# Local attention: one exponential more ahead of the copy of an older chunk's outputs on ScalarE

## The chip, the cores and the metric

The kernel runs on one core of a Trainium2 chip. The metric is device time in microseconds. The engines are called PE (TensorE, matmuls; its weight loads are listed as PEld), DVE (VectorE), ACT (ScalarE), POOL (GpSimd) and SP (SyncE).

## The reference

A small two-layer network on 4 images. The first stage (`tok`) makes 1024 tokens of 64 features per image by a short Fourier transform of patches. Then come local attention, a mixture of experts, full attention over each image, and a second mixture with a capacity, each after a layernorm and added to the stream. Only local attention matters here, per image:

```python
q = x @ wq.T                      # 16 heads of 64
kv = x @ wkv.T                    # one head of keys and values
k, v = (kv[..., :64], kv[..., 64:])
q = _rmsnorm(_rope(q), q_norm_w)
k = _rmsnorm(_rope(k), k_norm_w)
mask = (cols <= rows) & (rows - cols <= 128)
scores = jnp.einsum('bqgtd,bqgsd->bqgts', q, k) / sqrt(64)
scores = jnp.where(mask[None, None, None], scores, NEG)
attn = jax.nn.softmax(scores, axis=-1)
out = jnp.einsum('bqgts,bqgsd->bqgtd', attn, v)
return out.transpose(0, 3, 1, 2, 4).reshape(Bx, Tx, 1024) @ wo.T
```

## The kernel before

Each engine has its own written-out program, and engines wait for each other through counting semaphores; nothing is planned by a scheduler. The stages are setup, then for each of the 4 images `project` and `windowed` as one stage, then `experts`, `full` and `finish`. A barrier of all engines stands between stages.

`windowed` does local attention. The 1024 tokens of an image are cut into 32 chunks of 32 query rows. A chunk sees 160 keys (its own 32 and the 128 before). The 16 heads are handled as 4 groups q = 0 to 3 of 4 heads, so that a chunk's scores are 4 tiles of 128 x 160 in two PSUM banks, banks 0 and 1 for even chunks and 2 and 3 for odd ones. What the engines do in a chunk:

- PE, `scores` (L645 the mask, L649 the products): writes the chunk's scores. It waits until all four exponentials of the chunk two before are done, since they read the same banks (L634).
- DVE, L739 and L742: the maximum of each row, then the bias of the exponential from it (`bias_ready`). ACT waits for the bias at L789.
- ACT, L796: four ACTIVATEs with Exp, one per q, from PSUM to `probs`. Each also sums its row, and each is followed in the trace by an ACTIVATION_READ_ACCUMULATOR that stores the sum and counts up `exp_done`.
- DVE, L759: the reciprocal of the four sums, when all four exponentials are done. POOL, L775 and L777: the probabilities multiplied by it (`scaled`).
- PE, `turn` (L667): transposes the probabilities, of the 128 older keys and of the 32 own ones. It works on the chunk three before the one whose scores were just made. DVE, L751, copies them out of PSUM (`pT_ready`); the last three chunks are shared by DVE (L755) and ACT (L804).
- PE, `values` (L684 for the older keys, L681 for the own ones): the products with the values, in banks 6 and 7, four chunks behind the scores. It counts up `pv_done`. Before it writes the two banks for chunk c, it waits for `oT_ready` to reach c (L673), i.e. for the copy of chunk c - 1's outputs.
- ACT, `outputs` (L784): the copy of a chunk's outputs from banks 6 and 7 to `oT` in SBUF. It waits for `pv_done` (L783) and counts up `oT_ready`. Within ACT's slot for chunk c it copies chunk c - 4.

The order of the work is that of the programs. PE goes over n = 0 to 35 with scores(n), turn(n - 3), values(n - 4), in this order. DVE goes over n with maximum and bias of chunk n, the copy of the transposed chunk n - 3, the reciprocal of chunk n - 1. ACT goes over the chunks with its four exponentials, and from chunk 4 on with one copy between two of them. After ACT's loop, the outputs of the last four chunks are copied one by one (L800 to L805). Then PE multiplies all outputs by `wo` (L715), and the stage ends with transposes and additions. The loads of local attention's data are done by then, and the loop issues no DMA.

ACT's loop, with the placement of the copy at L793 and L794:

```python
for c in range(CHUNKS):
    a.wait_ge(S["bias_ready"], c + 1)
    if c >= 3:
        a.wait_ge(S["transposed"], c - 2)
    for q in range(NQ):
        if q == 2 and c >= 4:
            outputs(c - 4)
        e, hh = divmod(q, 2)
        nc.scalar.activation(probs[:, c % 3, q, :], ...
```

Of the kernel before, what the change touches and what calls it, by code (L numbers as in the profile page):

```python
# [80 lines left out]
def program(nc, inp, out_rows, sent_rows):  # L81
    with ExitStack() as ctx:
# [205 lines left out]
        def turned_scalar(a, at):  # L288

            a.wait_ge(S["xT_psum"], 1)  # L290
            nc.scalar.activation(xT[:, 0:HALF // 2], bank[at][:, 0:HALF // 2], ACT.Copy)
# [322 lines left out]
        def turned_half(c, r):  # L614

            return pT[:, c % 2, :].rearrange("p (q r t) -> p r q t", r=2, t=D)[:, r]

        def bank_of_half(r):

            return bank[4 + r][:, 0:(NQ + 1) * D].rearrange("p (q t) -> p q t", t=D)  # L620

        def windowed(block, b):
# [157 lines left out]
            @block.scalar  # L780
            def _(a):
                def outputs(c):
                    a.wait_ge(S["pv_done"], c + 1)  # L783
                    nc.scalar.activation(oT[:, :, CHUNK * c:CHUNK * (c + 1)].rearrange("p (h a) t -> p h a t", h=2),  # L784
                                         ps[:, 6:8, 0:P].rearrange("p h (a t) -> p h a t", t=CHUNK),
                                         ACT.Copy).then_inc(S["oT_ready"], 1)

                for c in range(CHUNKS):
                    a.wait_ge(S["bias_ready"], c + 1)  # L789
                    if c >= 3:  # L790
                        a.wait_ge(S["transposed"], c - 2)
                    for q in range(NQ):
                        if q == 2 and c >= 4:  # L793
                            outputs(c - 4)  # L794
                        e, hh = divmod(q, 2)
                        nc.scalar.activation(probs[:, c % 3, q, :],  # L796
                                             bank[2 * (c % 2) + e][:, SPAN * hh:SPAN * hh + SPAN], ACT.Exp,
                                             bias=small[:, c % 4, 1, q:q + 1], scale=rq[:, c, e, hh:hh + 1],
                                             accum_out=small[:, c % 4, 2, q:q + 1]).then_inc(S["exp_done"], 1)
                for c in range(CHUNKS - 4, CHUNKS):  # L800
                    if c + 1 < CHUNKS:
                        a.wait_ge(S["transposed"], c + 2)
                        a.wait_ge(S["pv_done"], c)
                        nc.scalar.activation(turned_half(c + 1, 1), bank_of_half(1), ACT.Copy).then_inc(S["pTr_ready"], 1)  # L804
                    outputs(c)  # L805
                a.wait_ge(S["out_done"], 1)
                nc.scalar.activation(outT, bank[0][:], ACT.Copy).then_inc(S["out_kept"], 1)
                if b + 1 < IMAGES:
                    turned_scalar(a, 1)
# [866 lines left out]
```

## Time and profile before

| | us |
|---|---|
| median of 3 runs | 902.27 (901.76 to 904.99) |
| the profiled execution | 902.57 |
| its span | 900.6 |
| PE busy | 728.4 (81%) |
| DVE busy | 606.4 (67%) |
| ACT busy | 449.2 (50%) |
| POOL busy | 429.0 (48%) |
| loop of local attention, image 0, first to last exponential | 84.1 to 153.4 |
| last exponential of image 3 | 519.4 |

The loop of local attention stands four times in the span, once per image. Busy times are sums of an engine's records, and records can overlap. Busy PE time is modelled and says little of how near PE is to its peak. Times in a timeline are from the start of the span.

### The profile page before, as it was taken

The page shows a single profiled execution, that of the slowest core. Times are in us where ns is not written, and L with a number is a line of the kernel's source. Part 1 is how long each engine was busy: PE and PEld are TensorE (multiplying, and loading weights), DVE is VectorE, ACT ScalarE, POOL GpSimd, SP SyncE. Part 2 cuts the span into 40 slices and gives each one's busy share as a digit, 9 for nine tenths or more (in the row PEclk, how much of TensorE's full clock was granted, in tenths as well). Part 3 has the DMA queues.
Part 4 walks back from the last instruction along what each step waited for, and adds up shares of the span by engine and source line. Part 5 has one row for each costly group of instructions (what it writes and reads, how often), then busy time and mean ns, then how long its engine had stood idle before and what let it go on. Part 6 is the DMA issues. An engine that isn't in the chain of part 4 may idle for free. (4 is left out here: it accounts for less than half of the span.)

```text
span 900.6 us, 21152 instructions
## 1 busy us (share of the span) xinstructions
PE 728.4 (81%) x8196; PEld 474.9 (53%) x8196; DVE 606.4 (67%) x1209; ACT 449.2 (50%) x1405; POOL 429.0 (48%) x556
## 2 busy tenths in 40 slices
PE   6699999899998989988689979987899986405850
PEld 6243776436774447764267734773577763403630
DVE  0378887598884988876878836676577759421980
ACT  0024999228993359972299925311666650201100
POOL 0655665275662656643656612662033230472675
PEclk9989999999999999999999998997999997556975
DMA  6453000170000810001200000008000004017000
GB/s 234 137 201 77 3 3 3 69 209 2 3 3 1 239 38 3 2 3 31 60 2 3 3 1 1 2 2 112 7 3 2 2 2 130 25 47 129 9 20 14
DMA packets 60009, 41.31 MB, mean 46 GB/s; under 512 B 51760, under 2 KB 57389, under 8 KB 59124
## 3 DMA queue, kind: packets, MB, share of 16 engines
q1 hardware_dynamic: 57462, 33.03, 14.6%
q10 hardware_dynamic: 144, 4.19, 1.2%
q0 software_dynamic: 2304, 2.74, 0.9%
q8 instruction: 66, 1.08, 0.5%
q14 instruction: 33, 0.27, 0.1%
HBM read 25.44 MB, written 7.15 MB: 36 GB/s over the span
## 5 line engine op out<-in xcount | busy, mean ns | idle before, releaser
L796 ACT ACTIVATE work<-ps,small,rq 128x160 f32<-128x160 f32 x512 | 243.3, 487 | 32.3 <-DVE small L742 31.8
L775 POOL TENSOR_TENSOR work<-work,small 128x512 f32<-128x512 f32 x128 | 133.3, 1041 | 123.6 <-DVE small L759 123.6
L739 DVE TENSOR_REDUCE ps<-ps 128x4 f32<-128x640 f32 x128 | 106.5, 832 | 40.6 <-PE ps L649 39.0
L796 ACT ACTIVATION_READ_ACCUMULATOR work<-ps,small,rq 128x1 f32 x512 | 105.2, 205 | 0.0
L649 PE MATMUL ps<-kT,big 64*128 64x160 f32 x1024 | 97.9, 311 | 0.0
L751 DVE COPY pT<-ps 128x640 f32<-128x640 f32 x116 | 95.5, 824 | 0.5 <-issue 0.5
L684 PE MATMUL ps<-pT,vwin 128*64 128x128 f32 x1024 | 84.2, 282 | 10.1 <-ACT big L784 2.4
L273 PE MATMUL ps<-xT,s_proj_w 64*128 64x512 f32 x288 | 76.9, 650 | 13.3 <-PEq L213 7.5
L609 POOL TENSOR_TENSOR big<-prod 128x1024 f32<-128x1024 f32 x28 | 65.8, 2362 | 26.2 <-DVE prod L576 26.0
L649 PEld LDWEIGHTS ps<-kT,big 64*128 64x128 f32 x1024 | 76.1, 191 | 0.1
L684 PEld LDWEIGHTS ps<-pT,vwin 128*64 128x64 f32 x1024 | 56.7, 136 | 24.0 <-issue 20.0
L526 ACT ACTIVATE big<-ps 128x1024 f32<-128x1024 f32 x32 | 32.8, 1024 | 62.5 <-DVE prod L576 57.5
L1561 POOL DMA_INDIRECT out<-big x40 | 44.0, 1100 | 32.4 <-DVE big L1531 20.5
L667 PE MATMUL ps<-s_ident,work 64*128 64x64 f32 x1024 | 55.3, 226 | 3.2 <-DVE pT L751 2.5
L681 PE MATMUL ps<-pT,vrem 32*64 32x128 f32 x1024 | 57.3, 293 | 0.0
L273 PEld LDWEIGHTS ps<-xT,s_proj_w 64*128 64x128 f32 x288 | 28.0, 197 | 53.4 <-issue 28.9
L1175 DVE TENSOR_REDUCE h<-ps 128x1 f32<-128x1024 f32 x32 | 39.1, 1225 | 23.1 <-PE ps L1082 23.1
L784 ACT ACTIVATE big<-ps 128x256 f32<-128x256 f32 x128 | 48.7, 380 | 10.6 <-PE ps L681 10.6
L1554 POOL DMA_INDIRECT sent_rows<-big,xb x32 | 31.5, 986 | 43.7 <-DVEq L1505 34.3
L667 PEld LDWEIGHTS ps<-s_ident,work 64*128 64x128 f32 x1024 | 47.8, 139 | 8.1 <-POOL pTr_own L777 4.2
L777 POOL TENSOR_TENSOR pTr_own<-work,small 128x128 f32<-128x128 f32 x128 | 51.3, 401 | 0.0
L1207 POOL TENSOR_TENSOR sum_off<-sum_off,hl 128x64 f32<-128x64 f32 x32 | 10.3, 321 | 79.9 <-DVE hl L1195 79.8
(284 smaller groups left out, 1407.0 us busy)
## 6 DMA issues: line engine op xcount, KB each, us to landing
xb<-in_x SPq DMA_DIRECT2D x3, 4096.0 KB, 13.2
xb<-in_x ACTq DMA_DIRECT2D x1, 4096.0 KB, 17.7
vrem<-hl SPq DMA_DIRECT2D x64, 64.0 KB, 2.1
sent_rows<-empty_row SPq DMA_DIRECT2D x8, 325.0 KB
s_proj_w<-in_proj_w SPq DMA_DIRECT2D x1, 1536.0 KB, 6.3
big<-sent_rows SPq DMA_DIRECT2D x5, 264.0 KB, 5.2
big<-sent_rows SPq DMA_DIRECT2D x5, 256.0 KB, 4.5
xb<-in_ffn_w SPq DMA_DIRECT2D x1, 1028.0 KB, 4.7
```

Source lines behind the costliest of these rows:

```text
L273: ins = nc.tensor.matmul(bank[banks + w][:], proj_w[half_rows(w), cols], xT[half_rows(w), :], start=True, stop=True)
L609: g.tensor_tensor(dst, first, second, ALU.add).then_inc(S["rot_done"], 1)
L649: ins = nc.tensor.matmul(tiles[e][:, hh, :], qT[half_rows(e), c, 4 * hh:4 * hh + 4, :].rearrange("p a t -> p (a t)"), kT[half_rows(e), CHU ...
L667: ins = nc.tensor.transpose(bank[4 + r][:, D * q:D * q + D], src, ident[half_rows(r), half_rows(r)])
L681: ins = nc.tensor.matmul(o, vrem[r, c, :], pT[r, c % 2, NQ * P:], start=False, stop=True, tile_position=(CHUNK * q, D * e), skip_group_che ...
L684: nc.tensor.matmul(o, vwin[:, c, :], pT[:, c % 2, P * q:P * q + P], start=True, stop=True, skip_group_check=True)
L739: ch.step(v.tensor_reduce(row_max(c), ps[:, s_banks(c), 0:2 * SPAN].rearrange("p e (h k) -> p e h k", h=2), X, ALU.max))
L751: v.tensor_copy(pT[:, c % 2, :].rearrange("p (q r t) -> p r q t", r=2, t=D), ps[:, 4:6, 0:(NQ + 1) * D].rearrange("p r (q t) -> p r q t", ...
L775: g.tensor_tensor(probs[:, c % 3, :, 0:P], probs[:, c % 3, :, 0:P], bc(small[:, c % 4, 3, :], P), ALU.mult)
L777: g.tensor_tensor(own[:, c % 2, :].rearrange("p (q k) -> p q k", q=NQ), probs[:, c % 3, :, P:SPAN], bc(small[:, c % 4, 3, :], CHUNK), ALU. ...
L784: nc.scalar.activation(oT[:, :, CHUNK * c:CHUNK * (c + 1)].rearrange("p (h a) t -> p h a t", h=2), ps[:, 6:8, 0:P].rearrange("p h (a t) -> ...
L796: nc.scalar.activation(probs[:, c % 3, q, :], bank[2 * (c % 2) + e][:, SPAN * hh:SPAN * hh + SPAN], ACT.Exp, bias=small[:, c % 4, 1, q:q + ...
```

## The change

The copy of chunk c - 4's outputs moves within ACT's slot for chunk c: it stood between the second and the third exponential and now stands between the third and the fourth.

```diff
                     for q in range(NQ):
-                        if q == 2 and c >= 4:
+                        if q == 3 and c >= 4:
                             outputs(c - 4)
                         e, hh = divmod(q, 2)
```

`outputs`, its wait and its count are unchanged, and so are all other engines' programs.

## Rows read from the trace of the kernel before

**Rows 1.** The page: PE's granted clock in 40 slices, tenths.

```profile
PEclk9989999999999999999999998997999997556975
```

**Rows 2.** Busy time by stretch; PE, PEld, DVE, ACT, POOL (instructions), PEclk, DMA share, GB/s.

```profile
96.00:149.00 53.00, 51.52 (x876) 40.09 (x876) 44.17 (x99) 53.00 (x219) 33.98 (x50) 1.00 0.01 2
```

**Rows 3.** Who waited for whom, 96 to 149 us: total, times, longest.

```profile
DVE ps L739 <- PE ps L649: 8.4, 25, 0.5
...
PEld ps L645 <- ACT work L796: 4.1, 24, 0.2
```

**Rows 4.** Timeline of image 0's loop: start, us, engine and line; [idle before, releaser].

```profile
116.46 0.10 PEld L645 LDWEIGHTS ps<-window_mask,row_of_t 64*128 64x128 bf16 x2 [0.17 <-ACT work L796]
...
117.12 0.38 ACT L784 ACTIVATE big<-ps 128x256 f32<-128x256 f32 x1
...
117.32 0.14 PEld L667 LDWEIGHTS ps<-s_ident,pTr_own 64*128 64x128 f32 x2
...
117.38 0.49 ACT L796 ACTIVATE work<-ps,small,rq 128x160 f32<-128x160 f32 x1
...
117.61 0.45 PEld L684 LDWEIGHTS ps<-pT,vwin 128*64 128x64 f32 x8
...
117.84 0.49 ACT L796 ACTIVATE work<-ps,small,rq 128x160 f32<-128x160 f32 x1
...
118.21 0.22 ACT L796 ACTIVATION_READ_ACCUMULATOR work<-ps,small,rq 128x1 f32 x1
118.22 0.21 PEld L681 LDWEIGHTS ps<-pT,vrem 32*64 32x64 f32 x8 [0.17 <-issue]
...
118.60 0.10 PEld L645 LDWEIGHTS ps<-window_mask,row_of_t 64*128 64x128 bf16 x2 [0.17 <-ACT work L796]
...
119.35 0.38 ACT L784 ACTIVATE big<-ps 128x256 f32<-128x256 f32 x1
...
120.35 0.16 DVE L742 SCALAR_TENSOR_TENSOR small<-ps,rq 128x4 f32<-128x4 f32 x1
...
120.55 0.49 ACT L796 ACTIVATE work<-ps,small,rq 128x160 f32<-128x160 f32 x1
...
121.49 0.38 ACT L784 ACTIVATE big<-ps 128x256 f32<-128x256 f32 x1
```

**Rows 5.** Timeline of the first chunks of image 0's loop, in the same columns.

```profile
89.96 0.21 ACT L796 ACTIVATION_READ_ACCUMULATOR work<-ps,small,rq 128x1 f32 x1
...
90.21 0.10 PEld L645 LDWEIGHTS ps<-window_mask,row_of_t 64*128 64x128 bf16 x2 [1.18 <-ACT work L796]
...
91.07 0.14 PEld L667 LDWEIGHTS ps<-s_ident,pTr_own 64*128 64x128 f32 x2
...
91.28 0.42 PEld L684 LDWEIGHTS ps<-pT,vwin 128*64 128x64 f32 x8
...
91.81 0.22 ACT L796 ACTIVATION_READ_ACCUMULATOR work<-ps,small,rq 128x1 f32 x1
...
91.86 0.21 PEld L681 LDWEIGHTS ps<-pT,vrem 32*64 32x64 f32 x8 [0.17 <-issue]
...
92.24 0.10 PEld L645 LDWEIGHTS ps<-window_mask,row_of_t 64*128 64x128 bf16 x2 [0.17 <-ACT work L796]
```

**Rows 6.** Timeline of the last chunks of image 0, in the same columns.

```profile
152.11 0.38 ACT L784 ACTIVATE big<-ps 128x256 f32<-128x256 f32 x1
...
152.60 0.45 PEld L684 LDWEIGHTS ps<-pT,vwin 128*64 128x64 f32 x8 [0.20 <-issue]
...
153.74 0.39 ACT L784 ACTIVATE big<-ps 128x256 f32<-128x256 f32 x1
153.86 0.36 PEld L667 LDWEIGHTS ps<-s_ident,work 64*128 64x128 f32 x8 [0.44 <-POOL pTr_own L777]
...
154.35 0.42 PEld L684 LDWEIGHTS ps<-pT,vwin 128*64 128x64 f32 x8
```

**Rows 7.** The line L784 over the whole trace: idle time before it (us, times).

```profile
  PE ps L681: 10.6, 13
```

## The prediction

> **What bounds the kernel now.** I went from the page to one stretch of local attention, and there from one handoff to the next.
>
> The page's clock line says that TensorE's clock was granted in full, but for a few dips, until the last third [rows 1]. The chain that ended last covers the final stage, so the question is what sets the pace of a chunk here. The stretch 96 to 149 us lies inside the chunk loop of image 0: ScalarE is busy 53.00 of 53.00 us, TensorE 51.52, VectorE 44.17 [rows 2]. ScalarE looks like the bound. But its records overlap (an accumulator read runs under the next ACTIVATE), so "full" can hide a wait of some hundredths. The chain of waits says so: 24 times the load for the next scores waited 0.17 us, and 25 times VectorE's maximum waited for the scores, 8.4 us in all [rows 3]. Something comes round in a ring.
>
> The timeline shows the ring [rows 4]. ScalarE's copy in chunk 15 (outputs of chunk 11) starts at 117.12 and takes 0.38, to 117.50. TensorE's values product starts at 117.61, 0.11 later; its loads end with L681's at 118.22 + 0.21 = 118.43. The scores of chunk 17 start at 118.60, 0.17 later; then come maximum and bias (120.35), chunk 17's first exponential at 120.55, 1.95 after the scores' start, and its copy at 121.49. From copy to copy over two chunks: 121.49 - 117.12 = **4.37 us** = 0.38 + 0.11 + 0.82 + 0.17 + 1.95 + 0.94. Each handoff begins when the one before ends.
>
> Two links could be chance, so I looked for each where it stands apart.
> - Copy to values. `values` waits for oT_ready of the chunk before, i.e. for the copy. The first one of an image has no copy before it, and its load follows the last transposing load by 0.07 (91.07 + 0.14 to 91.28) [rows 5]. In the loop that gap is 0.15 (117.32 + 0.14 to 117.61) and ends 0.11 after the copy [rows 4]; so it does at the image's end (152.11 + 0.38 to 152.60) [rows 6]. The copy ends this wait, by some 0.08 us.
> - Values to scores. At 118.60 both possible releasers ended together: L681's loads at 118.43, and the fourth exponential's accumulator read at 118.21 + 0.22 = 118.43 [rows 4]. The profile names the exponential. The loop's head parts them: where only the exponential is awaited, the scores' load starts about 0.05 after it (89.96 + 0.21 to 90.21); at 92.24 it starts 0.21 after the exponential (92.03) and again 0.17 after L681's loads (92.07) [rows 5]. So the 0.17 belongs to the products before, the ring goes through the copy, and the ring of the exponentials alone has 0.12 us to spare.
>
> **The change part by part.** It removes and adds no instruction. 28 copies per image (chunks 4 to 31), 112 in all, go behind the third exponential; the last four of each image, after the loop, stay. The moved step issues no DMA and passes no queue; only ScalarE's order changes.
>
> 1. The third exponential starts where the copy did, and the copy one exponential later. That step is 117.84 - 117.38 = 0.46 us [rows 4]. The fourth exponential starts and ends as before, since the same work stands before it. Worth 0: nothing waits for the third alone, the scores and the reciprocal wait for all four.
> 2. The copy's own wait for its product. The product whose loads end at 118.43 is copied at 119.35 [rows 4]; before this line ScalarE sat idle only 13 times of 128, 10.6 us in all [rows 7], nearly all of it behind the loop. No wait comes and none goes: 0.
> 3. The copy ends 0.46 later after its chunk's first exponential, so the next values product starts 0.46 later. Queued behind it on TensorE are the scores of the chunk after, with no slack at the 0.17 link. VectorE's maximum, the bias and the first exponential follow at the same 1.95, each waiting for the one before; VectorE idles before its maximum already [rows 3]. A round of the ring grows from 4.37 to **4.83 us**, a chunk from 2.19 to 2.42.
> 4. What is late next: the transposing products stand before the values in TensorE's order. They end 1.00 after the scores' start (116.46 to 117.46) [rows 4] and could let the values go 0.07 later, at 1.07; the values now start at 1.15 and will at 1.43. That leaves 0.36 us, so they don't matter; the gap is new idle time of TensorE.
> 5. How many rounds: chunk 4's copy delays chunk 6's scores, 6's delays 8's, up to 28's and 30's; the odd chunks likewise from 5 to 31. That is **13 rounds on each side**, interleaved and not added. 13 x 0.464 (the 0.46 with a little for the steps of 0.48 among them) = 6.03 us per image.
> 6. The end of the image. The last copy in the loop (152.11) also moves by 0.46, so the values at 152.60 go to 153.07, their copy from 153.74 to 154.20, and the transposes at 153.86 wait for the values' loads (153.07 + 0.82 + 0.17 = 154.06). The next values start 0.11 after the copy's end at 154.59, so at 154.70 instead of 154.35 [rows 6]. What follows is serial: 0.35 per image.
>
> Sum: 4 x (6.03 + 0.35) = **25.5 us**. The term that could be off is a round's growth. At the top 0.48, the longest step between exponentials: 4 x (6.24 + 0.35) = 26.4. At the bottom, if the 0.17 were the exponential's release and the scores could follow the values' loads with no gap, 0.46 - 0.17 = 0.29: 4 x (3.77 + 0.2) = 15.9.
>
> The profiled execution took 902.57 us with a span of 900.6, 2.0 around it, and stands 0.3 above the median of 902.27. By its own time the sum is 928.1; by the median **927.8**. I take 0.464 and not the bottom, because its row at 92.24 is a direct reading.
>
> Between two groups of loads on different rows of the array the timeline shows 0.17, from L684 to L681 and from L681 to the scores. The Trainium skill (TensorE: Matmul & The Clock Gate, "The mechanism" in Part 3) says that weight loads are pulled ahead of matmuls in flight when row groups don't conflict. By that rule the scores' loads would slip in under the values' matmuls and the sum would lie near the bottom, 15.9; the gap of 0.17 at the one place where it can be told speaks for 25.5.
>
> **The rivals.**
> - *The link to the scores gives way*: the exponential, not the products, released them. For: both end at 118.43, and the profile names it. Against: the 0.21 at 92.24 [rows 5]. Time 902.3 + 15.9 = 918.2.
> - *ScalarE is the bound, and its order doesn't matter.* For: 53.00 of 53.00 us [rows 2]. As a mechanism: four exponentials and a copy cost the same in any order, so the chunk stays 2.19, time 902.3. Against: they need only 0.48 + 3 x 0.46 + 0.26 = 2.12 us, and each first exponential starts within 0.05 of the bias's end. The Trainium skill (Perfetto Trace Analysis, "Identifying the Most-Contended Engine") takes the engine of highest occupancy for the one to optimize, and for ScalarE calls occupancy a fair measure; that is this rival's reading.
> - *Faster: in the loop the copy stalls the third exponential*, hidden under the overlapping records. Moved back, it would find its product finished and the chunk shrink toward 2.13: 112 x 0.06 = 6.7 us less, 895.6. It decides from the point where the product ends less than 0.05 us before the copy. Against: its loads end 0.9 us before, and rows 7.
> - *The clock.* TensorE idles 0.23 us more per chunk. Its full clock held through the loop [rows 2]; the dips stand at image borders and at the end [rows 1]. Borders move by 6 us, so dips may come or go, a few us either way. If the lower level (1.2 GHz) took hold of a loop, the 0.82 and a part of the 1.95 would lengthen and the time pass 935. Nothing at these idle shares suggests it.
>
> **How the numbers follow.** Ring through the copy, at full growth: 86%. Link gives way: 6%. No change: 4%. Faster: 1%. Clock falls: 3%, with the forecast's sign. The range takes in the first two: 917 at the bottom (918.2 less 1 for dips), 931.5 at the top (902.3 + 26.4, and 3 for dips and the spread of the runs, whose highest is 904.99). A measurement tells about 0.5%, 4.5 us, from no change: faster 1%, same 4%, slower 95%.
>
> **What would show it.** In the loop: copy to copy 4.83 us over two chunks; values still 0.11 after the copy; scores still 0.17 after L681's loads, but 0.6 after the accumulator read; ScalarE waiting for the bias (L742) some 100 times at 0.15 to 0.2 us and busy below 95% of the stretch; L684 waiting for ACT L784 by some 0.4 us each; VectorE's wait before L739 up by 0.23 each. It is wrong if copy to copy stays 4.37 or is near 4.66, or if the time appears outside the loop.

## The result and the profile after

| | before | after |
|---|---|---|
| median, us (4 runs each) | 902.01 (901.44 to 904.99) | 927.81 (926.29 to 929.47) |
| profiled execution, us | 902.57 | 926.86 |
| its span, us | 900.6 | 924.0 |

The ratio is 1.028, with a 95% interval of 1.026 to 1.030: slower, by 25.8 us. The forecast was 927.8 us.

The same view as [rows 4], a stretch of image 0's loop after the change; the columns are start and duration in us, engine and line, and in brackets the idle time before and its releaser:

```profile
118.88 0.47 ACT L796 ACTIVATE work<-ps,small,rq 128x160 f32<-128x160 f32 x1
...
119.14 0.10 PEld L645 LDWEIGHTS ps<-window_mask,row_of_t 64*128 64x128 bf16 x2 [0.17 <-ACT work L796]
...
119.80 0.38 ACT L784 ACTIVATE big<-ps 128x256 f32<-128x256 f32 x1
...
120.29 0.45 PEld L684 LDWEIGHTS ps<-pT,vwin 128*64 128x64 f32 x8
...
120.43 0.22 ACT L796 ACTIVATION_READ_ACCUMULATOR work<-ps,small,rq 128x1 f32 x1
...
120.91 0.21 PEld L681 LDWEIGHTS ps<-pT,vrem 32*64 32x64 f32 x8 [0.17 <-issue]
...
121.09 0.48 ACT L796 ACTIVATE work<-ps,small,rq 128x160 f32<-128x160 f32 x1 [0.45 <-DVE small L742]
...
121.29 0.10 PEld L645 LDWEIGHTS ps<-window_mask,row_of_t 64*128 64x128 bf16 x2 [0.17 <-issue]
...
122.49 0.38 ACT L784 ACTIVATE big<-ps 128x256 f32<-128x256 f32 x1
...
122.99 0.45 PEld L684 LDWEIGHTS ps<-pT,vwin 128*64 128x64 f32 x8 [0.66 <-issue]
...
123.12 0.22 ACT L796 ACTIVATION_READ_ACCUMULATOR work<-ps,small,rq 128x1 f32 x1
...
123.23 0.48 ACT L796 ACTIVATE work<-ps,small,rq 128x160 f32<-128x160 f32 x1
...
123.98 0.10 PEld L645 LDWEIGHTS ps<-window_mask,row_of_t 64*128 64x128 bf16 x2 [0.17 <-ACT work L796]
...
124.64 0.38 ACT L784 ACTIVATE big<-ps 128x256 f32<-128x256 f32 x1
```

Read it as a ring. The copy at 119.80 ends at 120.18; the values start 0.11 later at 120.29; their loads end at 120.91 + 0.21 = 121.12; the scores start 0.17 later at 121.29. By then the fourth exponential's accumulator read had been over since 120.65, for 0.64 us. The chunk's first exponential starts at 123.23, 1.94 after the scores, and its copy at 124.64, another 1.41 later. Copy to copy over two chunks is 124.64 - 119.80 = 4.84 us = 0.38 + 0.11 + 0.83 + 0.17 + 1.94 + 1.41, where it was 4.37 [rows 4]. Every link has its old length to within 0.01 us but the last one, from first exponential to copy, which was 0.94. The profile still names the exponential as releaser of the scores at 123.98, although its accumulator read was over at 123.12 + 0.22 = 123.34, 0.64 us before: with several waits, the releaser that is named need not be the one that counts.

The next rows cover the same stretch of 53 us as [rows 2] and [rows 3]: busy us of PE, PEld, DVE, ACT and POOL, then clock and DMA; below it who waited for whom (total, times, longest). The third block is for the copy's line over the whole trace, as in [rows 7]: ScalarE's idle time before it, and who waited for it (us, times). The last line is the same wait in the kernel before.

```profile
96.00:149.00 53.00, 46.55 (x792) 36.26 (x790) 39.89 (x88) 48.08 (x198) 30.40 (x45) 1.00 0.01 2
```

```profile
DVE ps L739 <- PE ps L649: 12.5, 22, 1.0
...
PE ps L684 <- ACT big L784: 6.0, 11, 0.6
ACT work L796 <- DVE small L742: 4.9, 11, 0.5
```

```profile
  PE ps L681: 12.9, 16
who waited for it (us, times):
  PE ps L684: 32.3, 60
```

```profile
  PE ps L684: 2.4, 4
```

ScalarE is busy 48.08 of 53 us and no longer looks full. It waits for the bias 11 times at 0.45 us, and TensorE waits for the copy (L684 <- L784) 60 times in the whole trace, 32.3 us in all, where it was 4 times and 2.4 us before, once at the end of each image.

From the start of image 0's first exponential to the start of its last the loop took 68.73 us before (84.11 to 152.84) and takes 74.77 now:

```profile
84.00 0.48 ACT L796 ACTIVATE work<-ps,small,rq 128x160 f32<-128x160 f32 x1 [7.24 <-DVE small L742]
...
158.77 0.49 ACT L796 ACTIVATE work<-ps,small,rq 128x160 f32<-128x160 f32 x1
```

That is 6.04 us more. (The 153.4 and the 519.4 of the table before the change belong to the accumulator reads of those last exponentials; by starts they are 152.84 and 519.0.) The four images' loops in the two traces, counted in this way, and the last copy of an image behind its last exponential:

| | before, us | after, us | more |
|---|---|---|---|
| loop of image 0 | 68.73 | 74.77 | 6.04 |
| loop of image 1 | 68.89 | 74.73 | 5.84 |
| loop of image 2 | 68.70 | 74.72 | 6.02 |
| loop of image 3 | 69.25 | 77.27 | 8.02 |
| last exponential to last copy, images 0 to 2 | 5.87 or 5.88 | 6.25 or 6.26 | 0.38 |
| the same, image 3 | 5.99 | 6.25 | 0.26 |

### The profile page after: what moved, and what is told of

Its sections match the earlier page's. It is cut to its first block and busy times, and to the rows that moved or that the text cites. A ratio compares the mean times of both kernels' runs of the same rounds, so it can differ in the third digit from the quotient of the medians.

```text
span 924.0 us, 21152 instructions
## 1 busy us (share of the span) xinstructions
PE 732.5 (79%) x8196; PEld 480.4 (52%) x8196; DVE 606.1 (66%) x1209; ACT 449.9 (49%) x1405; POOL 427.6 (46%) x556
## 5 line engine op out<-in xcount | busy, mean ns | idle before, releaser
L796 ACT ACTIVATE work<-ps,small,rq 128x160 f32<-128x160 f32 x512 | 243.5, 484 | 55.9 <-DVE small L742 55.5
L684 PE MATMUL ps<-pT,vwin 128*64 128x128 f32 x1024 | 84.7, 283 | 37.1 <-ACT big L784 32.3
L273 PE MATMUL ps<-xT,s_proj_w 64*128 64x512 f32 x288 | 76.9, 650 | 13.3 <-PEq L213 7.5
L684 PEld LDWEIGHTS ps<-pT,vwin 128*64 128x64 f32 x1024 | 57.2, 137 | 51.3 <-issue 46.2
L681 PE MATMUL ps<-pT,vrem 32*64 32x128 f32 x1024 | 57.6, 294 | 0.0
L784 ACT ACTIVATE big<-ps 128x256 f32<-128x256 f32 x128 | 49.1, 384 | 12.9 <-PE ps L681 12.9
L576 DVE TENSOR_TENSOR prod<-ps,s_rope_cos 128x1024 f32<-128x1024 f32 x32 | 39.0, 1219 | 13.4 <-PE ps L273 11.7
```

The lines of the kernel that those rows point to most:

```text
L273: ins = nc.tensor.matmul(bank[banks + w][:], proj_w[half_rows(w), cols], xT[half_rows(w), :], start=True, stop=True)
L681: ins = nc.tensor.matmul(o, vrem[r, c, :], pT[r, c % 2, NQ * P:], start=False, stop=True, tile_position=(CHUNK * q, D * e), skip_group_che ...
L684: nc.tensor.matmul(o, vwin[:, c, :], pT[:, c % 2, P * q:P * q + P], start=True, stop=True, skip_group_check=True)
L796: nc.scalar.activation(probs[:, c % 3, q, :], bank[2 * (c % 2) + e][:, SPAN * hh:SPAN * hh + SPAN], ACT.Exp, bias=small[:, c % 4, 1, q:q + ...
```

## The experiments

The theory: the pace is set by a ring from ScalarE's copy over the values and the scores, behind them in TensorE's order, back to ScalarE. Its rivals: the exponentials' own release of the scores; ScalarE's amount of work; a fixed price per moved copy; the amount of TensorE's work. Periods below are copy to copy over two chunks, read off the timeline of image 0's loop.

### One place earlier

```diff
-                        if q == 2 and c >= 4:
+                        if q == 1 and c >= 4:
```

> The copy stands between the first and the second exponential, one place earlier than in the kernel before. Ring through the copy: that ring would shrink by 0.46 to 3.91 us per two chunks, so the next ring binds. It is the one of the exponentials: 1.95 from the scores' start to the first exponential, 1.67 to the fourth, 0.59 to the end of its accumulator read, 0.05 to the next scores: 4.25 us. 13 x 0.12 x 4 = 6 us less: about 896 us. The scores then start 0.05 after the accumulator read. If the exponential is what released the scores with 0.17 in the kernel before: the ring stays 4.37 and the time 902. If only ScalarE's work counts: 902 too.

Measured: ratio 0.995 (0.992 to 0.998); median 905.7 beside 909.3 for the kernel before on that chip. The timeline of this kernel's loop:

```profile
116.21 0.40 ACT L784 ACTIVATE big<-ps 128x256 f32<-128x256 f32 x1
...
116.80 0.17 PEld L667 LDWEIGHTS ps<-s_ident,pTr_own 64*128 64x128 f32 x2
...
117.05 0.42 PEld L684 LDWEIGHTS ps<-pT,vwin 128*64 128x64 f32 x8
...
117.40 0.53 ACT L796 ACTIVATE work<-ps,small,rq 128x160 f32<-128x160 f32 x1
...
117.63 0.21 PEld L681 LDWEIGHTS ps<-pT,vrem 32*64 32x64 f32 x8 [0.17 <-issue]
...
117.77 0.25 ACT L796 ACTIVATION_READ_ACCUMULATOR work<-ps,small,rq 128x1 f32 x1
...
118.07 0.10 PEld L645 LDWEIGHTS ps<-window_mask,row_of_t 64*128 64x128 bf16 x2 [0.23 <-ACT work L796]
...
120.49 0.40 ACT L784 ACTIVATE big<-ps 128x256 f32<-128x256 f32 x1
```

The scores start 0.05 after the accumulator read (118.02 to 118.07) and 0.23 after L681's loads (117.84). So the exponential now releases them, and it takes 0.05 to do so, not 0.17. The values follow the last transposing load by 0.08 (116.97 to 117.05) and wait for no copy. The period is 120.49 - 116.21 = 4.28 us against 4.25 expected: the first rival, which had the ring stay at 4.37, falls. The 0.03 lies in the fourth exponential and its read, 0.62 us here (117.40 to 118.02) and 0.59 in [rows 4]. A chunk now takes 2.14 us, 0.02 more than the 2.12 of ScalarE's own work, so this run parts the exponentials' ring from ScalarE's work by no more than that.

The gain, 3.7 us by the medians and 0.5% by the ratio, is smaller than the 6 us expected. The loops of images 0 to 2 are 1.28, 1.20 and 1.33 us shorter than in the kernel before, but that of image 3 is 0.92 longer (70.17 against 69.25). The last section shows why.

On another chip, beside two of the others:

> The kernel of e1_second once more, beside the changed kernel and e3's on one chip. By its loops (67.98 us against 69.22 in image 0) it should be 4 x 1.2 = 5 us shorter than the kernel before, 0.5%, and 30 us shorter than the changed kernel.

Measured: 0.9957 (0.994 to 0.9975), 899.5 us beside 902.3, some 3 to 4 us where 5 were expected. The expectation multiplied image 0's gain by four, and image 3's loop again did not share in it (70.12 us). The gain is small but clear of the noise, so this placement beats both kernels.

### Ahead of the first exponential

```diff
-                        if q == 2 and c >= 4:
+                        if q == 0 and c >= 4:
```

> The copy stands ahead of the first exponential. Ring through the copy: now the copy comes before its values product is done. The product of the same round ends 2.14 us after the scores' start and is seen 0.06 later, so the copy starts at 2.20 instead of being free at 1.95, and the first exponential at 2.46; from there 1.40 to the fourth, 0.59 and 0.05: 4.50 us per two chunks, 0.13 more than before: 13 x 0.13 x 4 = 7 us more, about 909. A plain rule that earlier is better would give 896 or less; a rule that ScalarE's order doesn't matter gives 902.

Measured: 1.015 (1.010 to 1.019), 923.9 us beside 909.3: longer, as expected, but by twice the size. The timeline:

```profile
118.04 0.38 ACT L784 ACTIVATE big<-ps 128x256 f32<-128x256 f32 x1
...
119.78 0.45 PE L681 MATMUL ps<-pT,vrem 32*64 32x128 f32 x8
119.88 0.16 DVE L742 SCALAR_TENSOR_TENSOR small<-ps,rq 128x4 f32<-128x4 f32 x1
...
120.37 0.38 ACT L784 ACTIVATE big<-ps 128x256 f32<-128x256 f32 x1
120.65 0.48 ACT L796 ACTIVATE work<-ps,small,rq 128x160 f32<-128x160 f32 x1
```

The bias is ready at 120.04, but the copy now stands in front of the exponential and waits for its product, whose modelled end is 120.23; it starts 0.14 after that, not the 0.06 that the expectation took from the end of an image; why is not shown. The period is 4.55 us (from 115.82 to 120.37; the chunk between starts its copy at 118.04), 0.18 over the kernel before. That gives 4 x 13 x 0.18 = 9.4 us of the 13.6 measured. The rest lies in the loops too: those of images 0 to 2 are 2.7 to 2.9 us longer than before (71.45 us in image 0), of which 13 rounds of 0.18 explain 2.3, and that of image 3 is 4.9 longer (74.16 against 69.25), 13.3 in all. "Earlier is better" holds only up to the point where the copied product is late.

### Behind the fourth exponential

```diff
-                        if q == 2 and c >= 4:
-                            outputs(c - 4)
...
+                    if c >= 4:
+                        outputs(c - 4)
```

> The copy stands behind the fourth exponential, one place later than in the changed kernel. Ring through the copy: 0.46 more again, 5.30 us per two chunks, so 4 x (13 x 0.93 + 0.7) = 51 us over the kernel before: 953. If the exponentials' ring were what grew, it would be shorter here, since the copy no longer stands ahead of the fourth: about 896 to 902. If it is ScalarE's work alone: 902, as in any order.

Measured: 967.0 us beside 909.3, 1.067 (1.061 to 1.073). The single runs spread from 958.7 to 973.3. The timeline:

```profile
114.72 0.39 ACT L784 ACTIVATE big<-ps 128x256 f32<-128x256 f32 x1
...
115.22 0.45 PEld L684 LDWEIGHTS ps<-pT,vwin 128*64 128x64 f32 x8 [1.12 <-issue]
...
116.22 0.10 PEld L645 LDWEIGHTS ps<-window_mask,row_of_t 64*128 64x128 bf16 x2 [0.17 <-ACT work L794]
...
120.03 0.39 ACT L784 ACTIVATE big<-ps 128x256 f32<-128x256 f32 x1
```

In this kernel the exponentials are L794. The next copy of the same ring starts at 120.03: 5.31 us, where 5.30 was expected. No copy stands between the first and the fourth exponential any more, so by the links of [rows 4] the ring of the exponentials is down to 1.95 + 1.40 + 0.59 + 0.05 = 3.99 us, and yet the time is the longest of all placements. So that ring and ScalarE's amount of work are both out. The total was higher than the loops explain, hence:

> The kernel of e3_behind once more. Its loops were 11.8 us longer per image, 47 us in all, and with the image's end about 50 (5.5%), but the time was 6.7% longer. If the rest was that chip's, the ratio is now near 1.055; if it belongs to the kernel (a clock lowered outside the loops, for one), it is again near 1.067 and the profile shows where.

Measured: 953.7 us beside 902.3, 1.056 (1.053 to 1.060), near the 1.055 that the loops and the images' ends give. The surplus of the first measurement is in part explained and in part open. Its profiled execution (958.7 us, 1.054 times the 909.3) has the same loops as this one (80.54 us in image 0), and behind image 3's last exponential it took 387.1 us against 381.0. The other kernels traced on that chip took 386.6 to 389.0 there as well, so those 6 us are the chip's, which fits the kernel before at 909.3 there and 902.3 here. They don't raise the ratio. What does are two executions of 972.65 and 973.32 us with a mean granted clock of 0.892, where the two shorter ones had 0.917 and 0.910. On the second chip one of four was of that kind (968.95 us at 0.893). None of them was traced, so whether this placement makes them more likely is not shown.

### The changed kernel on that chip

> The changed kernel itself, so that the placements are compared on one chip: loops 6.04 us longer per image than in the kernel before, 25 us in all, 1.028. Against e4_even_only's 1.024 it tells whether moving half of the copies costs all but the whole.

Measured: 928.25 us, 1.028 (1.026 to 1.031). The placements on one scale; the first row's ratio is from another chip:

| the copy stands | period, us | ratio to before |
|---|---|---|
| before the 1st | 4.55 | 1.015 |
| before the 2nd exponential | 4.28 | 0.996 |
| before the 3rd (the kernel before) | 4.37 | 1 |
| before the 4th (the change) | 4.84 | 1.028 |
| behind the 4th | 5.31 | 1.056 |

### Half of the move

```diff
-                        if q == 2 and c >= 4:
+                        if q == 3 - c % 2 and c >= 4:
```

> Only the copies in even chunks stand between the third and the fourth exponential, those in odd chunks stay between the second and the third: half of the move. Two rings run interleaved, one through the even and one through the odd chunks, and ScalarE takes the chunks in order, so the faster waits for the slower. Ring through the copy: the even ring grows to 4.84 and drags the odd one, so nearly the whole price is paid: 4 x 13 x 0.464 = 24 us, about 926. If each moved copy costs 0.23 us by itself, half of them cost half: 915.

Measured: 1.024 (1.020 to 1.028), 932.1 us beside 909.3. Rows of the timeline:

```profile
114.03 0.10 PEld L645 LDWEIGHTS ps<-window_mask,row_of_t 64*128 64x128 bf16 x2 [0.17 <-ACT work L796]
...
114.18 0.41 ACT L784 ACTIVATE big<-ps 128x256 f32<-128x256 f32 x1
...
114.88 0.15 PEld L667 LDWEIGHTS ps<-s_ident,pTr_own 64*128 64x128 f32 x2
...
115.10 0.42 PEld L684 LDWEIGHTS ps<-pT,vwin 128*64 128x64 f32 x8
...
115.97 0.48 ACT L796 ACTIVATE work<-ps,small,rq 128x160 f32<-128x160 f32 x1 [0.45 <-DVE small L742]
...
117.38 0.39 ACT L784 ACTIVATE big<-ps 128x256 f32<-128x256 f32 x1
...
119.03 0.41 ACT L784 ACTIVATE big<-ps 128x256 f32<-128x256 f32 x1
...
122.22 0.38 ACT L784 ACTIVATE big<-ps 128x256 f32<-128x256 f32 x1
```

Both parities run at the long period: the moved ones 122.22 - 117.38 = 4.84, the unmoved 119.03 - 114.18 = 4.85. A price per moved copy would have given 1.014. Image 0's loop takes 74.75 us, as with all copies moved (74.77). What stays away is the price at the image's end: chunk 31 is odd, its copy is not moved, and the last copy follows the last exponential by 5.91 us, near the 5.87 of the kernel before.

The expectation laid the dragging on ScalarE, which takes the chunks in order. The rows put most of it on TensorE. The unmoved copy of chunk 13 ends at 114.59, but the values start at 115.10, not 0.11 but 0.51 later, and 0.07 after the last transposing load (114.88 + 0.15 = 115.03). Those transposes stand behind the scores of 114.03 in TensorE's order, and the scores belong to the slower ring. That is 0.40 of the 0.47 us that the slower ring is longer. ScalarE's own order adds less than 0.1: the unmoved chunk 15 has its bias at 117.97 and starts its first exponential at 118.10, behind the fourth of chunk 14, where 0.04 behind the bias is the rule.

### Fewer products in the ring

In the changed kernel and in the kernel before, the same edit; the count `pv_done` moves to the last product that is left:

```diff
-                    for own_keys in range(2):
+                    for own_keys in range(1):
```

> The changed kernel, with the values products of the own keys (L681) left out, so the outputs lack the part of a chunk's own 32 keys. Ring through the copy: the products in the ring shrink from 0.82 to 0.45 us of loads, the ring from 4.84 to 4.46 us per two chunks (the 0.17 behind them taken as before): 13 x 0.38 x 4 = 20 us less than the changed kernel, about 908. If the products aren't in what binds, 928 stays; if the clock had fallen for idleness it would be worse still.

> The kernel before, with the same products (L681) left out, so the outputs lack the same part. Ring through the copy: here the ring through the copy falls to 3.99, but the exponentials' ring of 4.25 us then binds, so only 0.12 of the 0.38 us per two chunks is gained: 6 us, about 896, a third of what the same omission gives in the changed kernel. If both kernels were bound by TensorE's amount of work, both would gain the same, some 20 us.

Measured, on one chip: 905.1 us for the changed kernel without L681 and 894.2 for the kernel before without it, beside 902.5 for the kernel before whole; ratios 1.002 (1.000 to 1.004) and 0.993 (0.990 to 0.996). The timeline of the first:

```profile
115.28 0.38 ACT L784 ACTIVATE big<-ps 128x256 f32<-128x256 f32 x1
...
119.74 0.38 ACT L784 ACTIVATE big<-ps 128x256 f32<-128x256 f32 x1
```

and who waited for whom in the second, 96 to 149 us:

```profile
PEld ps L645 <- ACT work L796: 10.2, 24, 0.4
```

The first's period is 4.46, as expected. The changed kernel gains 927.8 - 905.1 = 22.7 us by the omission (20 expected; its whole version ran on other chips, at 927.8 and 928.3), the kernel before 8.3 (6 expected). In the kernel before, the load for the scores now waits 0.4 us for the exponential each time, where it was 0.17 [rows 3], and the period is 4.28 us (copies at 117.91 and 122.19), as with the copy one place earlier: the exponentials' ring took over. The same products are worth almost three times as much in one kernel as in the other, so it isn't the amount of TensorE's work that binds.

The totals also hold something that neither expectation priced: behind the last exponential of image 0 the last copy comes 1.55 us sooner in the changed kernel (4.70 for 6.25) and 1.13 sooner in the kernel before (4.74 for 5.87). In image 0's loop alone the omission is worth 4.95 us in the one (74.77 to 69.82; 13 x 0.38 = 4.94) and 1.30 in the other (68.73 to 67.43).

## Why the prediction was right, point by point

- **What bounds.** The ring through the copy was read off two links, copy to values (0.11) and values to scores (0.17). Both held unchanged after the move, and the moves one place earlier and one later changed the period as the ring has it. The doubtful link, where two releasers ended together at 118.43, was decided by the row at 92.24 [rows 5]; moving the copy earlier showed the exponential's release to be 0.05, and "the link gives way" fell.
- **Step 1 and 2**, no price for the third exponential nor for the copy's own wait: right. The idle count before L784 went from 13 to 16 times and from 10.6 to 12.9 us; the ends of the four images account for that, where the copy at 160.13 now waits 0.45 for its product.
- **Step 3**, a round from 4.37 to 4.83: measured 4.84.
- **Step 4**, what is late next: right that nothing came of it, wrong in its size. It spread a round's growth over two chunks and found 0.36 us of slack before the transposes would matter. The chunks do not come every 2.42 us: scores start at 119.14, 121.29 and 123.98, 2.15 and 2.69 apart. Each ring grew by itself, and all of the growth went into every second distance (2.14 and 2.23 before). The short distance may be what the loop's head had given the rings, whose first two copies are 2.10 apart; no run tested that. In the short half the values start 1.15 after the scores, as before, and the transposing loads end some 0.15 before them. So half of the chunks have the old slack of under 0.1 us and the others 0.6. The same averaging put ScalarE's wait for the bias at some 100 of 0.15 to 0.2 us; there is one in every second chunk, of 0.45, over the trace 23.7 us more than before (55.5 against 31.8) where 15 to 20 were forecast.
- **Step 5**, 13 rounds, both rings not added: 6.04, 5.84 and 6.02 us in images 0 to 2, 6.03 forecast. Half of the move costing nearly the whole shows the "not added".
- **Step 6**, 0.35 per image's end: 0.38 in images 0 to 2 and 0.26 in image 3, from the last exponential to the last copy.
- **The sum.** 25.5 forecast, 25.8 by the medians. The mechanism gives 6.0 us in each of three loops and 0.4 at the ends; that the total is met so closely is partly luck. The spans of the two traces differ by only 23.4 us. Image 3's loop grew by 8.02 us, 2.0 more than forecast, and against that the changed kernel is 2.35 us shorter behind the last exponential (900.6 - 519.0 against 924.0 - 544.75), and 1.2 us shorter between the loops of images 1 and 2 and of 2 and 3, ends not counted. The first goes with the stretch of lower clock shown in the last section; the prediction had named such dips without a sum. The stretch behind the last exponential took 380.6 us in the changed kernel's second trace, so part of the 2.35 is spread from one execution to the next.
- **ScalarE's full 53 us** were the misleading row. The Trainium skill (Perfetto Trace Analysis, "Identifying the Most-Contended Engine") ranks engines by occupancy. Here ScalarE's 53.00 of 53.00 us hid that a chunk took 2.19 us where its own work needs 2.12; with the copy one place earlier the period fell to 2.14 per chunk, and there occupancy and bound nearly agree.
- **Loads pulled ahead.** The Trainium skill (TensorE: Matmul & The Clock Gate, "The mechanism" in Part 3) has weight loads pulled ahead of matmuls in flight when they go to other row groups. The prediction repeated that condition but did not check it, and by the kernel's code it is not met: the last two products of L681 stand on rows 32 to 63 and 96 to 127, and the scores' first load goes to rows 0 to 63. So the gap of 0.17 us, here or in any run, does not speak against that rule. What the traces show is a slip of about 0.08 us: in the kernel before, the scores' load at 118.60 stands 0.17 behind L681's last load, but ahead of the modelled end of L681's matmuls at 118.68.

```profile
118.23 0.45 PE L681 MATMUL ps<-pT,vrem 32*64 32x128 f32 x8
```

## What to carry to other kernels

When two engines hand work to each other in fixed orders, price a moved instruction by what stands behind its waiter in the waiter's own queue, not by its engine's busy time: here ScalarE did the same work in the same time, and the scores two chunks on paid. An engine at 100% in the records may still be waiting under overlapping ones; follow one ring of handoffs and see whether its terms add up to the period. With rings interleaved through the same in-order engines, the slowest sets the pace of all, and an early placement pays only until the thing placed must itself wait.

## What was not expected of the hardware

Image 3's loop grew by 8.02 us where image 0's grew by 6.04. Busy time by stretch of the changed kernel at its head, in the columns of [rows 2]:

```profile
464.00:468.60 4.60, 0.98 (x16) 0.72 (x12) 3.87 (x11) 1.12 (x5) 0.00 (x0) 0.99 0.01 4
468.70:478.90 10.20, 8.30 (x76) 6.87 (x78) 4.88 (x12) 8.62 (x37) 5.48 (x8) 0.51 0.00 0
478.90:489.00 10.10, 8.97 (x158) 6.94 (x154) 7.47 (x17) 8.45 (x37) 5.25 (x8) 1.00 0.01 3
```

and of the kernel before:

```profile
447.50:451.90 4.40, 0.12 (x2) 0.13 (x4) 2.91 (x8) 2.15 (x9) 0.00 (x0) 1.00 0.00 0
451.90:455.30 3.40, 3.00 (x28) 2.56 (x28) 1.20 (x5) 2.64 (x13) 2.22 (x3) 0.50 0.00 0
```

In the last image TensorE has no tokens of a next one to make at the loop's head and is nearly idle for over 4 us. In both kernels its clock then fell to the lower level (1.2 GHz), for 3.4 us before and for 10.2 us after the change, and those stretches did half as many matmuls per us as the next. In the kept traces the length goes with the kernel and not with the execution or the chip. In the kernel before and in both traces of the one with the copy behind the fourth exponential the low stretch took about 3.4 us, and image 3's loop 0.5 to 0.6 us more than image 0's. In the changed kernel's trace and the seven others, two of which repeat a kernel on another chip, it took about 10 us, and image 3's loop 2.0 to 2.8 us more. So some 2 us of the change's price, and the part of the gain that the placement one exponential earlier lacks, go with a longer stretch of lower clock. The prediction had put such dips down as a few us either way, without saying which. What makes the stretch short or long is open: no experiment here steered it.
